# Routed tiles of a decoder block: gated values split before they are turned, half of the upper down weights copied on ScalarE, last sums regrouped

## The reference

```python
x = hidden_states.reshape(-1, 512)                       # 1024 tokens
scores = jax.nn.sigmoid(x @ gate_w.T) + bias
topk_w, topk_idx = jax.lax.top_k(scores, 4)              # 4 of 16 experts
topk_w = topk_w / (jnp.sum(topk_w, axis=-1, keepdims=True) + 1e-20)
cw = jnp.sum(jax.nn.one_hot(topk_idx, 16) * topk_w[..., None], axis=1)
z = jax.nn.silu(einsum('th,eih->eti', x, Wg)) * einsum('th,eih->eti', x, Wu)
out = einsum('eti,ehi->th', z * cw.T[:, :, None], Wd)    # I = 256
out = out + jax.nn.silu(x @ Sg.T) * (x @ Su.T) @ Sd.T
return hidden_states + out
```

## Time and profile before

| | |
|---|---|
| median of 3 runs | 824.53 us |
| profiled execution, its own time | 822.42 us |
| its span | 820.6 us |
| TensorE busy | 787.3 us, 96% of the span |
| VectorE, ScalarE, GpSimd busy | 73%, 60%, 67% |
| chain that ended last | TensorE 77%, VectorE 9%, ScalarE 4% |
| DMA | 138.9 MB, 169 GB/s |

### The profile page before, as it was taken

How to read it: one execution, slowest core, us unless ns; L and a number is a source line. 1 busy time by engine, 2 the same in 40 slices (tenths; PEclk the granted TensorE clock), 3 DMA queues, 4 the chain that set the end, 5 groups by cost and what they waited for, 6 DMA issues and landing times.

```text
span 820.6 us, 21111 instructions
## 1 busy us (share of the span) xinstructions
PE 787.3 (96%) x7645; PEld 439.8 (54%) x7645; DVE 598.9 (73%) x1026; ACT 491.4 (60%) x927; POOL 547.3 (67%) x428
## 2 busy tenths in 40 slices
PE   6689999999999999999999999989989999999997
PEld 2564645645645645645645645644545555555553
DVE  6897796595586686686686686798887666666678
ACT  3799987587587587587588478356323344433341
POOL 6953496796896796896796897933244556555541
PEclk9899999999999999999999999999999999999999
DMA  8029526416416516507506505545144557577893
GB/s 333 8 81 285 175 72 233 133 59 229 150 51 230 153 41 236 158 26 244 165 17 238 178 9 169 179 172 207 66 144 154 181 193 251 193 266 269 296 378 150
DMA packets 50660, 138.92 MB, mean 169 GB/s; under 512 B 6176, under 2 KB 8224, under 8 KB 46240
## 3 DMA queue, kind: packets, MB, share of 16 engines
q1 hardware_dynamic: 43600, 116.93, 42.7%
q0 software_dynamic: 6400, 20.98, 7.3%
q10 hardware_dynamic: 592, 0.08, 0.1%
HBM read 96.02 MB, written 39.85 MB: 166 GB/s over the span
## 4 chain that ended last, share of the span: by engine, by line
PE 77%; DVE 9%; ACT 4%; POOL 3%; DMA 2%; issue 2%; SPq 2%; DVEq 0%; ACTq 0%; POOLq 0%
PE ps L1732 46%; PE ps L2184 18%; PE ps L1953 3%; PE ps L2174 2%; PE ps L1939 2%; PE ps L2208 2%; PE ps L1894 1%; DMA w_split<-stage 1%; PE ps L2240 1%; SPq L450 1%; POOL ring_mem L609 1%; DVE reg_b L1213 1%; DMA ring_mem<-in_x_half 1%; DMA w_split<-reg_h 1%; DVE x_res L1687 1%
## 5 line engine op out<-in xcount | busy, mean ns | idle before, releaser
L1732 PE MATMUL ps<-wo_hi,reg_b 128*128 128x512 f16 x448 | 142.4, 379 | 0.2 <-DVE ring_mem L1277 0.2
L702 POOL DMA_INDIRECT y_rows<-reg_h,to_row x40 | 67.2, 1680 | 83.9 <-ACT reg_h L1110 81.9
L2184 PE MATMUL ps<-ring_mem,reg_h 128*64 x480 | 112.7, 385 | 4.0 <-DVE kv L1630 1.6
L661 POOL TENSOR_SCALAR reg_h<-reg_h 128x512 f32<-128x512 f32 x56 | 94.9, 1695 | 30.0 <-ACT reg_h L912 29.7
L2186 PE MATMUL ps<-kv,reg_h 128*64 128x512 f16 x480 | 112.8, 385 | 0.0
L665 POOL TENSOR_TENSOR reg_h<-reg_h 128x512 f16<-128x512 f32 x84 | 108.7, 1294 | 4.7
L1732 PE MATMUL ps<-hT_hi,wq_hi 128*128 128x512 f16 x256 | 97.1, 379 | 1.1 <-DVE ring_mem L1268 1.1
L1732 PE MATMUL ps<-hT_hi,wq_lo 128*128 128x512 f16 x256 | 97.0, 379 | 0.0
L1732 PE MATMUL ps<-hT_lo,wq_hi 128*128 128x512 f16 x256 | 97.0, 379 | 0.0
L623 POOL TENSOR_TENSOR ring_mem<-kv,ring_mem 128x512 f16<-128x512 f32 x64 | 80.3, 1254 | 23.2 <-ACT ring_mem L837 23.2
L1732 PE MATMUL ps<-wo_lo,reg_b 128*128 128x512 f16 x224 | 84.9, 379 | 0.0
(11 more groups left out here) (340 smaller groups left out, 2019.3 us busy)
## 6 DMA issues: line engine op xcount, KB each, us to landing
ring_mem<-w_split SPq DMA_DIRECT2D x16, 1536.0 KB
w_split<-reg_h SPq DMA_DIRECT2D x88, 256.0 KB, 2.1
reg_h<-in_wgu SPq DMA_DIRECT2D x58, 256.0 KB, 3.5
stage<-in_wq SPq DMA_DIRECT2D x8, 1024.0 KB, 8.1
stage<-in_wo SPq DMA_DIRECT2D x8, 1024.0 KB, 6.2
reg_h<-in_wd SPq DMA_DIRECT2D x30, 256.0 KB, 3.1
wkv_st<-in_wkv SPq DMA_DIRECT2D x8, 512.0 KB, 8.8
ring_mem<-in_x_half SPq DMA_DIRECT2D x8, 256.0 KB, 5.8
```

The costliest lines, as they stand in the source:

```text
L661: pool.tensor_scalar(st, st, WS, None, ALU.mult).then_inc(pre_scaled_pool, 1)
L702: pool.indirect_dma_start(y_rows, bass.IndirectOffsetOnAxis(ap=to_row[:, r - 1:r], axis=0), y[r % 2], None).then_inc(scattered[r % 2], 16)
L1732: last = pe.matmul(dst, lhsT(c), rhs(c), start=(m == 0), stop=(m == n - 1))
L2184: pe.matmul(dst[0:TS, :], x[:, 0:TS], ring[:, bass.ds(at + w, BANK)], start=(first and n == 0), stop=(stop and n == 2))
```

## The change

The gated values are split into a high and a low float16 part while they are still in slot order (`gated_hi`, `gated_lo` read `tz32` in SBUF), and both parts are then turned by TensorE in eight half-width float16 products (`turn_gated`) into one bank. `turn_gated(r - 1)` stands in the middle of `gate_up(r)`, before its third chunk of four. ScalarE copies the turned parts to SBUF in one instruction of 512 columns (`gated_turned`, new semaphore `zT_done`). ScalarE also copies the upper half's down weights of tiles 2 to 40, in two pieces of 1024 columns: piece 0 at the end of an iteration, piece 1 behind `gated_turned`; VectorE keeps the copy of tile 1. Piece copies wait for `upper_gate` of their tile; `gate_up` now waits for `upper_gate` alone. On ScalarE `gated_hi` moves ahead of `down_out`; on VectorE `slots_lo` moves ahead of `gated_up` in tiles 2 to 39, and `gated_lo` ahead of the sums in the middle. Of the last sums, those of tile 38 shrink from five to two and those of tiles 39 and 40 grow from six to nine; (7, 1) becomes a product of TensorE (11 instead of 10 in all), and `LAST_SUMS` and `STORE_ORDER` are put in another order. The semaphore `dve_consts` and its wait in `key_norm` go, and VectorE waits for its own write instead.

```diff
 BANK_SUM = -1
-PE_PICKS = {7: (3, 2), 5: (3, 2, 1, 0), 6: (3, 2, 1, 0)}
-MID_SUMS = {TILES - 2: ((0, 3), (1, 3)), TILES - 1: ((0, 2), (1, 2)), TILES: ((0, 1),)}
-EARLY_SUMS = {TILES - 2: ((2, 3), (3, 3), (4, 3)), TILES - 1: ((2, 2), (3, 2), (4, 2))}
-LAST_SUMS = ((1, 1), (2, 1), (3, 1), (4, 1), (7, BANK_SUM), (7, 1), (0, 0), (1, 0), (2, 0), (5, BANK_SUM), (3, 0), (4, 0),
-             (7, 0), (6, BANK_SUM))
+PE_PICKS = {7: (3, 2, 1), 5: (3, 2, 1, 0), 6: (3, 2, 1, 0)}
+MID_SUMS = {TILES - 2: ((0, 3), (1, 3)), TILES - 1: ((2, 3), (3, 3)), TILES: ((3, 2), (4, 2), (0, 1))}
+EARLY_SUMS = {TILES - 1: ((4, 3), (0, 2), (1, 2), (2, 2))}
+LAST_SUMS = ((1, 1), (2, 1), (3, 1), (4, 1), (0, 0), (7, BANK_SUM), (1, 0), (2, 0), (7, 0), (3, 0), (4, 0),
+             (5, BANK_SUM), (6, BANK_SUM))
 SUM_ORDER = tuple(itertools.chain(*(itertools.chain(MID_SUMS[r], EARLY_SUMS.get(r, ())) for r in sorted(MID_SUMS)),
...
 FACTOR_ORDER = tuple((t, k) for t in PE_PICKS for k in PE_PICKS[t])
-STORE_ORDER = (0, 1, 2, 5, 3, 4, 7, 6)
+STORE_ORDER = (0, 1, 2, 7, 3, 4, 5, 6)
 FACTORS_FROM = 8
...
         tz32 = pair(reg_h[:, 3584:4096], I)
-        zT_hi, zT_lo = ([w.bitcast(F16).rearrange("p (c s) -> p c s", c=IC) for w in pair(flat(wkv_st)[:, i:i + P * IC], P)]
-                        for i in (0, P * IC))
+        zT = [w.bitcast(F16).rearrange("p (z c s) -> p z c s", z=2, c=IC) for w in pair(flat(wkv_st)[:, 0:512], 256)]
+        tz = [w.bitcast(F16).rearrange("p (z i) -> p z i", z=2) for w in pair(flat(wkv_st)[:, 512:1024], 256)]
...
             sem("pre_hi"), sem("pre_scaled_act"), sem("pre_scaled_pool"), sem("pre_split_dve"), sem("pre_split"))
-        zeroed, consts, dve_consts = sem("zeroed"), sem("consts"), sem("dve_consts")
+        zeroed, consts = sem("zeroed"), sem("consts")
         chain = sem("chain")
...
         tT_ps, tT_hi_done, tT_lo_done = sem("tT_ps"), sem("tT_hi_done"), sem("tT_lo_done")
-        zT_ps = sem("zT_ps")
+        zT_ps, zT_done = sem("zT_ps"), sem("zT_done")
         td_ps, y_done = sem("td_ps"), sem("y_done")
...
             def gated_hi(r):
+                act.wait_ge(z32_done, SHARED_UNITS + r)
+                act.activation(tz[r % 2][:, 0, :], tz32[r % 2], ACT.Copy).then_inc(z_hi_done, 1)
+            def gated_turned(r):
                 act.wait_ge(zT_ps, r)
-                act.activation(zT_hi[r % 2], ps[:, 2 + r % 2, 0:IC * P].rearrange("p (c s) -> p c s", c=IC),
-                               ACT.Copy).then_inc(z_hi_done, 1)
+                act.activation(zT[r % 2], ps[:, 2 + r % 2, :].rearrange("p (z c s) -> p z c s", z=2, c=IC),
+                               ACT.Copy).then_inc(zT_done, 1)
...
+            def upper_place(r):
+                h = 2 * r - 1
+                return act.value_load(tab_int[0:1, h:h + 1], min_val=0, max_val=(RING - 1) * EXPERT)
+            def upper_down(r, at, c):
+                act.wait_ge(upper_loaded, 2 if r == 2 else r + 1)
+                item = 2 * BANK * (KC + c)
+                act.activation(upper_w[r % 2][:, item:item + 2 * BANK], ring[:, bass.ds(at + item, 2 * BANK)], ACT.Copy)
...
             act.activation(tT[1][:, 1, :, :], ps[:, 5, :].rearrange("p (k s) -> p k s", k=KC), ACT.Copy).then_inc(tT_lo_done, 1)
+            act.wait_ge(tables_done, 1)
+            upper_at = upper_place(2)
             for r in range(1, TILES + 1):
+                if r >= 2:
+                    gated_turned(r - 1)
+                    upper_down(r, upper_at, 1)
+                    if r < TILES:
+                        upper_at = upper_place(r + 1)
                 gated(r)
...
                     slots_hi(r + 1)
+                gated_hi(r)
                 if r >= 2:
                     down_out(r - 1)
-                gated_hi(r)
                 n = r - FACTORS_FROM
...
                     pick_factors(*FACTOR_ORDER[n])
+                if r < TILES:
+                    upper_down(r + 1, upper_at, 0)
+            gated_turned(TILES)
             down_out(TILES)
...
             dve.wait_ge(small_in, 80)
-            dve.tensor_tensor(wqk[:, :], norm_sb[:, 0:1], norm_sb[:, 1:2], ALU.mult).then_inc(dve_consts, 1)
+            then(dve.tensor_tensor(wqk[:, :], norm_sb[:, 0:1], norm_sb[:, 1:2], ALU.mult))
             normalise_rows(2, lambda n: h2[:, n, :], h2_dve)
...
                 dve.wait_ge(k32_done, ev(p, 2, th))
-                if th == 0:
-                    dve.wait_ge(dve_consts, 1)
                 dve.scalar_tensor_tensor(k32[:, th, :], k32[:, th, :], wqk[:, 0:1], rk[:, th, :],
...
             upper_gate(1, first_at, loads)
-            next_at, loads = upper_place(2)
+            second_at, loads = upper_place(2)
             for t in add_order[3:5]:
                 shared_add(t)
-            upper_gate(2, next_at, loads)
+            upper_gate(2, second_at, loads)
             shared_add(add_order[5])
...
                 dve.wait_ge(silu_done, SHARED_UNITS + r)
-                if r >= 3:
-                    dve.wait_ge(zT_ps, r - 2)
                 dve.scalar_tensor_tensor(tz32[r % 2], ps[:, r % 2, I:2 * I], 1.0 / WS, tsilu[r % 2],
...
                 dve.wait_ge(z_hi_done, SHARED_UNITS + r)
-                dve.tensor_tensor(zT_lo[r % 2], ps[:, 2 + r % 2, 0:IC * P].rearrange("p (c s) -> p c s", c=IC),
-                                  zT_hi[r % 2], ALU.subtract).then_inc(z_split, 1)
+                dve.tensor_tensor(tz[r % 2][:, 1, :], tz32[r % 2], tz[r % 2][:, 0, :], ALU.subtract).then_inc(z_split, 1)
...
             for r in range(1, TILES + 1):
+                if 1 < r < TILES:
+                    slots_lo(r + 1)
                 gated_up(r)
-                if r < TILES:
+                if r == 1:
                     slots_lo(r + 1)
+                gated_lo(r)
                 for t, k in MID_SUMS.get(r, ()):
                     token_sum(t, k)
-                gated_lo(r)
                 pick_weights(r)
...
                     dump_rows()
-                if r < TILES:
-                    upper_down(r + 1, next_at)
                 if r + 2 <= TILES:
                     upper_gate(r + 2, *following)
-                    next_at = following[0]
                 if r + 3 <= TILES:
...
+            def turn_gated(r):
+                pe.wait_ge(z_split, SHARED_UNITS + r)
+                if r <= 2:
+                    pe.wait_ge(d_added, 4 + r)
+                for z in range(2):
+                    for c in range(IC):
+                        for half in range(2):
+                            first = c * P + half * TS
+                            col = (z * IC + c) * P
+                            last = pe.matmul(ps[half * TS:half * TS + TS, 2 + r % 2, col:col + P],
+                                             tz[r % 2][:, z, first:first + TS], ident_h[:, :], start=True, stop=True)
+                last.then_inc(zT_ps, 1)
             def gate_up(r, at):
-                pe.wait_ge(upper_loaded, 2 * r - 1)
+                pe.wait_ge(upper_loaded, r if r <= 2 else r + 1)
                 pe.wait_ge(tT_hi_done, r)
...
                 for k in range(KC):
+                    if k == KC // 2 and r >= 2:
+                        turn_gated(r - 1)
                     last = half_products(r, ps[:, r % 2, :], hi[:, k, :], lo[:, k, :], k, at, k == 0, k == KC - 1)
...
-            def transpose_gated(r):
-                pe.wait_ge(z32_done, SHARED_UNITS + r)
-                if r <= 2:
-                    pe.wait_ge(d_added, 4 + r)
-                for c in range(IC):
-                    last = pe.transpose(ps[:, 2 + r % 2, c * P:(c + 1) * P], tz32[r % 2][:, c * P:(c + 1) * P],
-                                        ident[:, :])
-                last.then_inc(zT_ps, 1)
             def down(r, at):
-                pe.wait_ge(z_split, SHARED_UNITS + r)
+                pe.wait_ge(zT_done, r)
                 if r == 1:
...
                     pe.wait_ge(y_done, r - 2)
-                pe.wait_ge(upper_loaded, 2 * r)
+                if r == 1:
+                    pe.wait_ge(upper_loaded, 3)
                 for c in range(IC):
-                    last = half_products(r, ps[:, 6 + r % 2, :], zT_hi[r % 2][:, c, :], zT_lo[r % 2][:, c, :], KC + c, at,
+                    last = half_products(r, ps[:, 6 + r % 2, :], zT[r % 2][:, 0, c, :], zT[r % 2][:, 1, c, :], KC + c, at,
                                          c == 0, c == IC - 1)
...
                     down(r - 1, before_at)
-                transpose_gated(r)
                 before_at, now = now, ahead
...
             pick_product(*FACTOR_ORDER[0])
+            turn_gated(TILES)
             down(TILES, before_at)
...
```

## The result

The forecast was wrong in its sign. The changed kernel took 848.59 us (median of 4 runs, 846.93 to 848.87) beside 824.82 us of the kernel before, a ratio of 1.0256 (95% interval 1.018 to 1.0331). On a second chip it was 846.64 beside 826.05 us, 1.0261 (1.0179 to 1.0344). The profiled run took 848.80 us, its span 847.0.

A forecast was written before the change was run, and what follows sets the result against it. TensorE's instruction stream was taken as the bound. Span 820.6 - 3.1 (start) - 10.0 (36 tiles) + 0.7 (end) = 808.2 us; the median 824.53 minus 12.4 gave 812.1 us, range 809.8 to 818.

The forecast's parts named there:

- TensorE, per tile: Steady tiles: half-transposes at 0.22 us replace float32 transposes at 0.465, saving 0.26; tile 4.82 to 4.56 us.
- ScalarE, per tile: Steady tiles: ScalarE's instructions, with two pieces at 0.947 us, sum to 3.96 of 4.56 us and fit.
- Who waits for ScalarE: Steady tiles: waits on ScalarE and the slots covered by slacks of 0.4 to 0.9 us; no stall.
- the line on the steady tiles: 36 tiles at 4.56 us, 164.2 us where it was 174.2; 10.0 us gained.
- I set zero where ScalarE sees the turn's end: Start of the per-tile ScalarE timeline, put 0.21 us after TensorE goes on past the slots' turn.
- The start: Tiles 2 and 3 start earlier, at 614.0 and 618.9; 3.1 us gained, assuming the clock stays.
- The end: Last sum starts 22.0 us after tile 39's gate_up, 0.7 more; waits of 1.1 and 0.85 before down(40).
- the first rival: Clock falls around the turn before down(40), 1.7 us more: 813.8; at the start too, 815.3; chance 0.20.
- ScalarE did not become the bound: Rival on steady tiles: pieces over about 1.1 us make ScalarE the bound, 816 to 830 us; chance 0.12.
- The turn costs what was reckoned: Rival inside gate_up: the turn costs what it replaced, period near 4.8, 821 us; chance 0.06.
- The scatter's landing: Rival: down_out waits for GpSimd's scatter to land, 0.3 us each for five tiles, 813.6; chance 0.07.

The follow-up runs named there:

- e4: Changed kernel plus a GpSimd memset of 512 columns of unused memory, and its wait, between scatter and gather: 816.34 us, 0.9872 of the kernel before.
- u3: e3 with VectorE copying the upper half's down weights in one instruction and ScalarE copying no pieces: 821.88 us, 0.9962 of the kernel before.
- e3: Changed kernel with GpSimd's gather starting on the slots' turn's signal, ahead of the scatter of two tiles back: 816.86 us, 0.9866 of the kernel before.
- u1: Changed kernel with VectorE copying all down weights and ScalarE no pieces: 820.11 us, 0.9934 of the kernel before.
- x1: Kernel before with only GpSimd's commands exchanged, gather ahead of the scatter of two tiles back: 824.21 us, 0.9986 of the kernel before.
- l1: Changed kernel without the 36 gathers beside the tiles (result not the reference's): 815.65 us, 0.9888 of the kernel before.
- t1: e3 with the kernel before's last sums, TensorE products and store order: 818.95 us, 0.9932 of the kernel before.
- e2: Kernel before with GpSimd's order alone changed, the gather as soon as gate_up is done and the scatter behind it: 847.46 us, 1.0265.

## Why the prediction was wrong

*TensorE, per tile.* Right. The eight half-transposes take 0.22 us (700.97 to 701.19) and there is no seam around them. Without a gather the tile is 4.56, and in the stretch from 680 to 720 of e4 TensorE is busy all of 40 us:

```profile
680.00:720.00 40.00, 40.00 (x534) 24.02 (x532) 22.29 (x35) 37.00 (x67) 24.43 (x27) 1.00 0.65 228
```

*ScalarE, per tile.* Right: a piece is 1.05 long and followed in 0.94 to 0.95, `gated_hi` is 0.42 long where 0.38 was taken, and the engine is busy for 37.00 of 40 us in that row without being the bound. The Trainium skill (ScalarE: Activation LUTs, Rules for kernel authors) gives plain arithmetic to VectorE, and I weighed keeping the copies there by that rule. Here u3 against e3 shows no gain from it: with the copies on VectorE the kernel is slower, by some 3 us without the fallen clock, of which 1.5 are late increments again and the rest VectorE's queue at the two ends. ScalarE had room.

*Who waits for ScalarE.* This is the step that failed, and with it the line on the steady tiles. It counts from the zero of the paragraph ahead of it, "I set zero where ScalarE sees the turn's end, 0.21 after TensorE goes on", and so takes that 0.21 as fixed because two rows had it. It moves GpSimd's scatter, asks only whether it lands in time, and never asks where the gather behind it comes to lie. GpSimd was followed as a queue of transfers and not as an engine that is active beside a signal. Slack on the slots was put at 0.4 us; the delay is 1.1, and of the slack hardly anything was there to take it. In e4 `slots_lo` ends at 701.04 and the next `gate_up` starts at 701.43, 0.39 later, but 0.34 of that TensorE needs when it has stopped for the signal. That is why even the 0.08 of u1 and u3 cost 0.05 a tile. 29 tiles lost 1.03 to 1.36 us each and three more 0.25 to 0.45, and 36 tiles took 196.5 us where 164.2 were forecast and 164.1 measured without gathers.

The trace of before had it. In one of its early tiles the gather starts before the turn, and both readers are 0.8 us late:

```profile
644.26 0.61 PE L2174 MATMUL ps<-ident_h,hT_hi 128*64 128x128 f16 x16
```

```profile
645.72 0.60 ACT L1091 ACTIVATE reg_h<-ps 128x512 f16<-128x512 f32 x1 [0.49 <-PE ps L2174]
```

```profile
645.72 0.69 DVE L1662 CAST reg_h<-ps 128x512 f16<-128x512 f32 x1
```

```profile
642.76 0.99 POOL L702 DMA_INDIRECT y_rows<-reg_h,to_row  x1 [1.79 <-ACT reg_h L1110]
644.05 1.56 POOL L698 DMA_INDIRECT hT_hi<-h_rows,from_row  x1 [0.30 <-issue]
```

In the steady tiles of before the scatter lasted 1.81 us and the gather started 0.62 after the turn, just when the increment fell due. That 0.26 us later start (0.62 against 0.36) was all that kept it clear. Of the 0.8 us by which "the old 36 tiles exceeded 36 x 4.82" these early tiles were most: x1, where no such increment is late, takes 173.7 and not 174.2. I put them in the sum and didn't ask what they were.

*The start.* Right in direction and mostly in size. The clock stayed at 1.00. From the first turn to `gate_up(3)` it is 13.2 us in l1 and e4 (13.4 in the changed kernel) where it was 15.8: 2.6 gained, 3.1 forecast. The term is too large by 0.5, and most of that is one omission: it lets `gate_up` start 0.05 after `slots_lo` ends, but TensorE starts 0.35 after it. In the changed kernel:

```profile
618.91 0.68 DVE L1684 CAST reg_h<-ps 128x512 f16<-128x512 f32 x1
...
624.13 0.69 DVE L1684 CAST reg_h<-ps 128x512 f16<-128x512 f32 x1
```

These end at 619.59 and 624.82, and `gate_up` of tiles 2 and 3 starts at 619.94 and 625.17.

More than half of this gain is the clock's, and the kernel before doesn't lose it in every execution. In x1, which differs from it in GpSimd's order alone, TensorE waits before tile 2 as before, but the granted clock stays at 1.00 behind it where the earlier trace rows have 0.62, and the stretch takes 14.4 us. Against that the change gains 1.2. How often the kernel before loses the clock there is not known; it may be a part of why the medians below gain less than was forecast.

*The end.* 22.2 where 22.0 was forecast. The two waits before `down(40)` are 0.78 and 0.78 instead of 1.1 and 0.85. That it costs 0.9 more than before (21.3) is not the doing of the sums, as t1 shows (22.4 with the old ones).

*The sum without the collision.* From span 820.6: start -2.6, tiles -10.2, end +0.9 gives 808.7, where 808.2 was forecast; l1 has 810.2 with a first turn 1.6 us later. In medians e3 and e4 are 9.2 and 9.7 us under the kernel before of the same chip, where 12.4 were forecast. Their 36 tiles take 1.6 to 2.2 us more than 164.2, mostly in two or three tiles each in which `down_out` waited for a scatter's landing (1.9 us in two waits in e3, 3.0 in three in e4) or the commands behind came late and met the turn after all.

*The rivals.* The clock didn't fall in the changed kernel. In u3 it fell at the very place that the first rival names, around the turn before `down(40)`, and cost some 1.6 us where 1.7 were reckoned. ScalarE did not become the bound. The turn costs what was reckoned. The scatter's landing cost nothing in the changed kernel, and 48.3 us of waits on ScalarE in e2, where it starts later. None of the four was the cause, and the range, built from them, reached to 818. (Its lower end adds up to 810.0 and not 809.8.)

## What to carry to other kernels

When a change shifts an engine that issues indirect DMAs, place its commands on the same time line as the signals between the other engines, and look in the trace of before for tiles where the two meet. A reader that starts later than usual while its producer has gone on, beside a second idle reader that starts at the same instant, is a late signal and not a slow engine. And a chain with 0.4 us of slack on one signal has to be tested against the largest delay that this signal shows anywhere in the trace, not against its median. Here it was enough to let the gather start on the signal (e3), and not 0.3 us before it.
